# A two-stage image layer: offset matrices composed, k and v turned by VectorE, side work spread and a tile later, VectorE's large steps in halves

## The reference

```python
qkv  = conv1x1(layernorm(x), w_qkv)              # 3 x 128 channels
q, k, v = depthwise 3x3 filters of qkv           # w_dw, b_dw
for g in range(4):                               # groups of 32 channels
    y      = concat(conv3x3(q[:32], pconv_off_w[g]), q[32:])     # "pconv"
    off[g] = conv1x1(y, w_off[g], b_off[g])      # 9 taps x (dy, dx)
mask = sigmoid(conv1x1(pconv(q, pconv_mask_w), w_mask, b_mask))  # 9 taps
# per point, group and tap: k and v at (y + ky + dy, x + kx + dx), bilinear
# from 4 corners, times mask; then attention of q over the 9 taps, w_proj, + x
```

## Time and profile before

| | |
|---|---|
| time, median of 3 runs | 9839.31 us (9834.57 to 9847.19) |
| the profiled execution's own time | 9855.23 us |
| its span, first to last instruction | 9853.4 us |
| busy PE / DVE / ACT / POOL | 3062.5 / 5717.2 / 1524.3 / 4639.8 us |
| first stage (`first_layers` up to the last tile) | 0 to 7035 us |
| gathers issued (L512) | 4608, 4583.7 us busy |
| granted TensorE clock, mean | 0.637 of full speed |

### The profile page before, as it was taken

How to read it: one execution, slowest core, us unless ns; L and a number is a source line. 1 busy time by engine, 2 the same in 40 slices (tenths; PEclk the granted TensorE clock), 3 DMA queues, 4 the chain that set the end, 5 groups by cost and what they waited for, 6 DMA issues and landing times. The chain is left out here.

```text
span 9853.4 us, 106326 instructions
## 1 busy us (share of the span) xinstructions
PE 3062.5 (31%) x41476; PEld 2212.3 (22%) x41476; DVE 5717.2 (58%) x6511; ACT 1524.3 (15%) x3478; POOL 4639.8 (47%) x4747
## 2 busy tenths in 40 slices
PE   3102101021001001021001100111245476899997
PEld 2000000000001000010000000000224365788885
DVE  6486574765754456765754455544574465555554
ACT  1000000000000000000000000100122132444442
POOL 0776677665777557766777566765200000000000
PEclk7556555555555555555555555555577788999998
DMA  4433345332453224333453234332221532222224
GB/s 86 121 107 98 88 115 145 105 93 85 117 147 99 83 83 124 102 103 90 114 150 99 80 89 117 102 91 74 52 44 71 162 93 82 71 67 64 67 67 176
DMA packets 822918, 966.47 MB, mean 98 GB/s; under 512 B 283029, under 2 KB 643561, under 8 KB 817897
## 3 DMA queue, kind: packets, MB, share of 16 engines
q0 software_dynamic: 221184, 604.27, 20.7%
q1 hardware_dynamic: 573880, 321.25, 13.3%
q10 hardware_dynamic: 27440, 34.87, 1.0%
HBM read 797.64 MB, written 155.99 MB: 97 GB/s over the span
## 5 line engine op out<-in xcount | busy, mean ns | idle before, releaser
L512 POOL DMA_INDIRECT l_rec<-records,l_row x4608 | 4583.7, 995 | 2384.4 <-issue 1423.6
L673 PE MATMUL l_pso<-l_id,l_att_t 128*128 128x128 f32 x128 | 60.8, 475 | 4714.6 <-DVE l_att_t L1074 2549.4
L1056 DVE TENSOR_TENSOR l_rec<-l_rec,l_psv 128x4608 f32<-128x4608 f32 x128 | 634.0, 4953 | 1044.7 <-DMA l_rec<-records,l_row 892.4
L673 PEld LDWEIGHTS l_pso<-l_id,l_att_t 128*128 128x128 f32 x128 | 23.3, 182 | 4781.9 <-DVE l_att_t L1074 2585.9
L1074 DVE TENSOR_REDUCE l_att_t<-l_rec 128x128 f32<-128x4608 f32 x128 | 1004.2, 7845 | 4.4
L2329 DVE COPY l3p_mix<-l3p_ps 128x512 f32<-128x512 f32 x1024 | 659.8, 686 | 576.6 <-PE l3p_ps L2205 576.6
L2291 ACT ACTIVATE l3p_mix<-l3p_ps 128x512 f32<-128x512 f32 x1024 | 556.7, 596 | 663.9 <-PE l3p_ps L2205 663.9
L1057 DVE TENSOR_REDUCE l_psv<-l_rec 128x144 f32<-128x4608 f32 x128 | 635.0, 4961 | 4.4
L1072 DVE TENSOR_TENSOR l_rec<-l_rec,l_psv 128x4608 f32<-128x4608 f32 x128 | 634.0, 4953 | 6.0 <-issue 1.6
L2205 PE MATMUL l3p_ps<-l3p_psi,l3p_ms 32*128 32x128 f32 x16384 | 612.4, 283 | 21.2 <-DVE l3p_mix L2329 16.6
L2166 POOL COPY l3p_four<-l3p_fil 128x128 f32 (+1 forms) x64 | 18.7, 293 | 1198.9 <-PE l3p_psm L2258 1197.8
(11 more groups left out here) (358 smaller groups left out, 6120.4 us busy)
## 6 DMA issues: line engine op xcount, KB each, us to landing
l_rec<-records,l_row POOLq DMA_INDIRECT x4608
l2b_w<-l_w SPq DMA_DIRECT2D x32, 1024.0 KB, 10.9
records<-l_area SPq DMA_DIRECT2D x48, 512.0 KB
l_row<-meta SPq DMA_DIRECT2D x124, 154.0 KB
l_x_hat<-l3a_xout ACTq DMA_DIRECT2D x32, 512.0 KB, 4.4
l3p_xin<-l_x_hat SPq DMA_DIRECT2D x128, 128.0 KB, 3.1
l_y_raw<-l3p_yr SPq DMA_DIRECT2D x64, 256.0 KB, 3.0
l3p_yin<-l_y_raw SPq DMA_DIRECT2D x128, 128.0 KB, 2.9
```

The costliest lines, as they stand in the source:

```text
L512: pool.indirect_dma_start(out=rec[:, r, c % HT, :], out_offset=None, in_=records[b].rearrange("r c d -> r (c d)"), in_offset=bass.Indirect ...
L1056: step(dve.tensor_tensor(keys, keys, asked.broadcast_to([P, GROUPS, TAPS * CORNERS, HC]), ALU.mult))
```

## The change

- **Offset matrices.** The weights of the 3x3 convolution come in another layout (`wt_s`, `wt_m`), are multiplied once on TensorE by the 1x1 matrices (`effect`, `we_s`), and a job offc is now three matmuls with the composed matrix on the shifted q and one on q. off4 and offm are gone. offs is a transposing job in batch 0 too.
- **Blocks turned by VectorE.** k and v are no longer transposed by TensorE and copied by ScalarE; one VectorE transpose of 32 x 32 blocks each, over 128 x 4096 elements (`blocks_of`), writes `kv_t`. A partition then holds one x of 32 for a group of channels, and `keep` stores from 32 partitions (was 64) in a transfer, with pieces of the same 256 bytes.
- **At most two jobs a slot** in points (one slot, number 20, has three). PG is 46, LG 39.
- **A tile later.** ScalarE takes jobs two slots after TensorE; on TensorE the projection of tile t - 1 comes behind the value sum of tile t; ScalarE's `turned` is of t - 1 and its store of t - 2; VectorE adds t - 2 and waits for the transpose of t - 1 in its place; SP loads the residual a turn later. linear's own steps move by one or two slots.
- **Halves of 18.** Each large step of VectorE is two, over two groups of channels (18 of the 36 records). GpSimd waits for each half of the values by itself before it issues 18 gathers.

```diff
-        opening = [("qkv", (f, g), 5 + f) for f in range(3) for g in range(NG)]
...
-        beside = [("qkv", (f, g), 5 + (NG * f + g) // 6) for f in range(3) for g in range(NG)]
-        beside += [("qt", g, 18 + g // 3) for g in range(NG)]
-        beside += [("off4", g, 21 + g // 3) for g in range(NG)] + [("offm", g, 21 + (NG + g) // 3) for g in range(NG)]
-        beside += [("offc", g, 28 + g // 4) for g in range(NG)] + [("offs", g, 30 + g // 4) for g in range(NG)]
-        beside += sorted([("kt", g, 39 + g // 2) for g in range(NG)] + [("vt", g, 38 + g) for g in range(NG)], key=lambda j: j[2])
+        alone = [("qkv", (f, g), 5 + f) for f in range(3) for g in range(NG)]
+        alone += [("qt", g, 17) for g in range(NG)] + [("offc", g, 20) for g in range(NG)] + [("offs", g, 28) for g in range(NG)]
+        beside = [("qkv", (f, g), 5 + (NG * f + g) // 2) for f in range(3) for g in range(NG)]
+        beside += sorted([("qt", g, 17 + g // 2) for g in range(NG)] + [("offc", g, 20 + g) for g in range(NG)], key=lambda j: j[2])
+        beside += [("offs", g, 28 + g // 2) for g in range(NG)]
...
-                    y0 = 1 - dy + half
-                    dst = cells_of(b)[g, y0:y0 + H - 1:2, 1:1 + W, dy, :].rearrange("t x d -> x t d")
-                    src = kept[W * half:W * half + W, :, g, :, :].rearrange("p t a d -> p t (a d)")
+                    x0 = 1 + HC * half
+                    dst = cells_of(b)[g, 1 - dy:1 - dy + H, x0:x0 + HC, dy, :].rearrange("y x d -> x y d")
+                    src = kept[HC * g:HC * g + HC, half:NT * CORNERS:2, :, :].rearrange("p y a d -> p y (a d)")
...
-                if 2 <= t < TILES + 2:
-                    r = t - 2
+                if t >= 3:
+                    r = t - 3
...
             for b in range(BATCH):
                 with pool.Fori(max(1, b * NT // AHEAD), (b + 1) * NT // AHEAD) as i:
                     for s in range(AHEAD):
                         hold(pool, s_row[s], 16 * i + 16, s_gate[1])
-                        hold(pool, s_dve, AHEAD * STEPS * (i - 1) + summed(s + 2), s_gate[1])
-                        gather(b, s)
+                        for h in range(2):
+                            hold(pool, s_dve, AHEAD * STEPS * (i - 1) + summed(s + 2, h), s_gate[1])
+                            half(b, s, h)
...
                             for dy in range(3):
-                                last = pe.matmul(bank[0:m, :], wp_s[:, dy, o:o + m], pads[0][0:3 * HC, 8 * at + dy:8 * at + dy + 8, 0:W],
-                                                 start=dy == 0, stop=dy == 2)
...
+                                pe.matmul(o, we_s[:, dy, :], pads[0][0:3 * HC, 8 * at + dy:8 * at + dy + 8, 0:W], start=dy == 0, stop=False)
                             last = pe.matmul(o, wc_s[:, :], q_img[:, at * 512:at * 512 + 512], start=False, stop=True)
...
                 pe.wait_ge(s_dve, summed(t))
+                if t >= 1:
+                    project(t - 1)
                 pe.transpose(ps_a, att_t[t % 2][:, :], id_s[:, :]).then_inc(s_att, 1)
-                project(t)
...
-                        if own + int(b >= 1 and kind != "qkv") != slot or kind == "offs":
+                        if own + 2 * int(b >= 1) != slot or kind == "offs":
...
                 weigh(t)
+                if t >= 2:
+                    store(t - 2)
                 if t >= 1:
-                    store(t - 1)
-                turned(t)
+                    turned(t - 1)
...
+                def blocks_of(f):
+                    kept = kv_t if b else kv_t0
+                    dve.transpose(kept[:, :, f - 1, :], img[f].rearrange("p (j s) -> p j s", s=HC)).then_inc(a_blk, 1)
...
-                    for f, at in ((0, 10), (1, 18), (2, 37)):
+                    for f, slots in ((0, range(9, 17)), (1, range(18, 26)), (2, (30, 31, 32, 33, 39, 40, 41, 42))):
...
+                    if slot == 43 and b:
+                        dve.wait_ge(a_mst, b * 32 + 32)
+                        blocks_of(1)
+                    if slot == 44 and b:
+                        blocks_of(2)
...
             def add(t, step):
-                dve.wait_ge(s_proj, t + 1)
+                if t + 1 < TILES:
+                    dve.wait_ge(s_att, t + 2)
+                else:
+                    dve.wait_ge(s_proj, t + 1)
...
                 for h in range(2):
+                    keys = view[h][:, :, :, 0:HC]
+                    asked = ps_q[:, HG * HC * h:HG * HC * (h + 1)].rearrange("p (g o d) -> p g o d", o=1, d=HC)
                     dve.wait_ge(s_rec[2 * two + h], 16 * HT * (t // 2 + 1))
-                step(dve.tensor_tensor(keys, keys, asked.broadcast_to([P, GROUPS, TAPS * CORNERS, HC]), ALU.mult))
+                    step(dve.tensor_tensor(keys, keys, asked.broadcast_to([P, HG, TAPS * CORNERS, HC]), ALU.mult))
...
-                if t >= 1:
-                    add(t - 1, step)
+                if t >= 2:
+                    add(t - 2, step)
...
+                for h in range(2):
+                    values = view[h][:, :, :, HC:2 * HC]
+                    part = ps_w[:, HT * CORNERS * h:HT * CORNERS * (h + 1)].rearrange("p (g m) -> p g m", g=HG)
+                    step(dve.tensor_tensor(values, values, part.unsqueeze(3).broadcast_to([P, HG, TAPS * CORNERS, HC]), ALU.mult))
+                    dve.tensor_reduce(att_t[two][:, HG * HC * h:HG * HC * (h + 1)].rearrange("p (g d) -> p g d", g=HG),
+                                      values.rearrange("p g m d -> p g d m"), AX, ALU.add).then_inc(s_dve, 1)
```

More of the change, by code:

```diff
@@ L334, in taken, with after @@
             return sum(1 for j in jobs[:n] if j[0] != "offs")
-        def after(jobs, kind):
-            return max(n for n, j in enumerate(jobs) if j[0] == kind) + 1
+        def after(jobs, kind, at=NG - 1):
+            return [j[0:2] for j in jobs].index((kind, at)) + 1
         lj = [("x", g, 3 + g // 3) for g in range(NG)] + [("k", g, 10 + g // 4) for g in range(NG)]
@@ L571, in points @@
                             for t in range(4):
                                 i = 4 * at + t
-                                last = pe.transpose(bank[:, t * P:t * P + P], src[:, i * P:i * P + P], id_s[:, :])
-                        if kind in ("off4", "offm"):
+                                last = pe.transpose(bank[:, t * P:t * P + P], q_img[:, i * P:i * P + P], id_s[:, :])
+                        if kind == "offc":
                             if at == 0:
                                 pe.wait_ge(a_shift, b * 48 + 64)
-                            m, o = (P, 0) if kind == "off4" else (HC, P)
+                                pe.wait_ge(a_eff, 1)
+                            o = bank[0:OFFS, :]
@@ L578, in points @@
                             for dy in range(3):
-                                last = pe.matmul(bank[0:m, :], wp_s[:, dy, o:o + m], pads[0][0:3 * HC, 8 * at + dy:8 * at + dy + 8, 0:W],
-                                                 start=dy == 0, stop=dy == 2)
-                        if kind == "offc":
-                            pe.wait_ge(a_act, done_act + taken(pj, after(pj, "offm")))
-                            o = bank[0:OFFS, :]
-                            pe.matmul(o, wa_s[:, :], conv4[:, at * 512:at * 512 + 512], start=True, stop=False)
+                                pe.matmul(o, we_s[:, dy, :], pads[0][0:3 * HC, 8 * at + dy:8 * at + dy + 8, 0:W], start=dy == 0, stop=False)
@@ L585, in points @@
                             last = pe.matmul(o, wc_s[:, :], q_img[:, at * 512:at * 512 + 512], start=False, stop=True)
-                        if kind == "offs" and b:
-                            pe.wait_ge(a_act, done_act + taken(pj, pj.index(("offc", at, 28 + at // 4)) + 1))
+                        if kind == "offs":
+                            pe.wait_ge(a_act, done_act + taken(pj, after(pj, "offc", at)))
                             for t in range(4):
@@ L590, in points @@
                                 last = pe.transpose(bank[:, t * P:t * P + OFFS], conv4[0:OFFS, i * P:i * P + P], id_s[0:OFFS, 0:OFFS])
-                        if kind == "offs" and not b:
-                            pe.wait_ge(a_act, done_act + taken(pj, after(pj, "offm")))
-                            for t in range(4):
-                                i = 4 * at + t
-                                o = bank[:, t * P:t * P + OFFS]
-                                pe.matmul(o, conv4[:, i * P:i * P + P], wa_s[:, :], start=True, stop=False)
-                                last = pe.matmul(o, q_img[:, i * P:i * P + P], wc_s[:, :], start=False, stop=True)
                         last.then_inc(a_job, 1)
@@ L743, in linear @@
                     for n, (kind, g, own) in enumerate(lj):
-                        if own + 1 != slot:
+                        if own + 2 != slot:
                             continue
```

236 lines of the change are left out of this document (120 added, 116 removed).

## The result

The changed kernel takes 9594.93 us in the median of 4 runs (9577.43 to 9633.59), the kernel before 9841.13 (9834.57 to 9847.19) beside it: ratio 0.9755, 95% interval 0.9725 to 0.9786. It is faster, by 2.45%. Forecast were 9490 us and a gain of 353; the medians give 246. The profiled execution took 9595.74 us with a span of 9593.5, so 260 us of span went, against 353 forecast.

What follows compares the result with a forecast made beforehand. GpSimd's gathers bound the first stage, with waits on VectorE from TensorE's per-instruction pace. Terms of -300, -110, +10, +70, +2 and -25 sum to -353, giving 9502 profiled and 9490 us as median; 8 in 10: 9220 to 9700.

Steps and rivals of the forecast that it cites:

- What bounds the kernel: First stage: GpSimd's gathers set a floor of 45.0 us a tile, 5760 us; TensorE's slow jobs hold VectorE up.
- Composed matrices and turned blocks, two a slot: Points batches: less TensorE work per tile cuts GpSimd's waits from 359.6 to 60 us, -300, bounds -150 and -360.
- Halves: Linear batches: GpSimd's next gather released 6.4 us earlier at each of 18 waits, 115 us, booked as -110.
- Everything a tile later in linear: Linear batches: better order but the same TensorE work, so given nothing; bounds 0 and -280.
- Four more steps a tile: VectorE's split steps cost 0 to 0.8 us a tile, partly hidden by idle time: +10, up to +97.
- What the faster VectorE uncovers: Gathers stopped beside VectorE's side steps and block transposes, in three batches: +70, bounds 0 and +107.
- rival C: GpSimd's gathers take 1.40 us instead of 1.25 when issued without pauses: +113, 9950 us; chance 0.06.
- Block transposes: Two a batch on VectorE, about 4.4 us each, up to 7.85; without a lock +55 instead of +70.
- Start: Before the first gather: two transposes, 8.8 us instead of 6.9, +2, up to +9; stores at worst +25.
- End: After the last gather: the last tile needs some 25 us instead of 65; -25, bounds 0 and -40.
- A: TensorE's pace came from ping-pong with ScalarE, so all 744.8 us of waits go: 9150 us; chance 0.15.
- B: TensorE stays the bound in points and linear batches; waits move to VectorE's `add`: -123, 9715 us; chance 0.23.

Runs made afterwards that it cites:

- six_a_slot_b: Changed kernel with the qkv jobs six a slot again, where the kernel before took 9845.58 us: 9606.72 us, ratio 0.9755.
- whole_steps_b: Changed kernel with VectorE's four large steps a tile whole again, where the kernel before took 9837.7 us: 9593.91 us, ratio 0.9745.
- six_a_slot: Changed kernel with the qkv jobs six a slot again, where the kernel before took 8867.17 us: 8867.81 us, ratio 1.0000.
- tiles_alone: Changed kernel with other batches' side work moved behind the tiles, gathering batch 0's records only, where the kernel before took 8867.17 us: 10022.92 us.
- after_again: The changed kernel, unchanged, run once more where the kernel before took 9845.0 us: 9625.38 us, ratio 0.9764.
- before_again: The kernel before, unchanged, run once more for its trace where the kernel before took 9845.0 us: 9842.85 us, ratio 1.0001.
- tiles_alone_b: Changed kernel with other batches' side work moved behind the tiles, gathering batch 0's records only, where the kernel before took 9837.7 us: 10677.24 us.

## Why the prediction was right in direction and 105 us off

The time fell into the likeliest case's range (9350 to 9620), in part by luck: the waits in the points fell by 60 us more than forecast, those in the linear batches by the size forecast but not for the reason given, and the gathers cost three times their term (238 against 80). On a chip B no run of a variant gained anything. By its own steps:

- **What bounds the kernel: half right.** TensorE's slow jobs under gathers do hold VectorE up on chips A. But the floor of 45.0 us a tile, 5760 us in all, was read from the median gather, and on a chip A it is not reachable: with everything else taken away the gathers need 6421. Before stood 330 us above that (6751.1), after stands 94 above it (6515.2). Even 6421 is no hard floor: pauses earn pace back, so waits and pace can't simply be added to it.
- **Composed matrices and turned blocks, two a slot: -300.** The points' waits went from 359.6 us to nothing, the end of the bounds (-360). The offc tiles, feared for 45 to 67 us of jobs, wait nowhere. Undoing the two jobs a slot for qkv brings no wait back (six_a_slot_b), so the cause is the smaller work, the tile of slack, the spreading of the other jobs, or several of these; the two runs that were to tell the first two apart met the other kind of chip.
- **Halves: -110, measured 0.** This is the term that failed. The linear waits did fall by 385.2 - 270.9 = 114.3, the size forecast, but they stand at 270.2 with whole steps too (whole_steps_b), so it wasn't the halves. And a shorter wait would not have shortened the stage by its length: on a chip A pauses of 24 us are paid back to nine tenths (671 of 747 us). I had priced the earlier release at its full length, and not asked what a pause gives.
- **Everything a tile later in linear: 0.** By elimination the 114 us belong here or to the work taken away; no run shows which.
- **Four more steps a tile: +10.** With whole steps the time is the same, within some 20 us, and the run takes away gain and cost together. The instructions themselves cost what was bounded: two half steps take 5.10 us for 4.95 (L1068, L1056) and 8.00 for 7.85 (L1089, L1074), 0.15 us each, some 0.6 a tile. VectorE's idle time, with 1525.7 us of waits for the gathers' data, can cover that.
- **What the faster VectorE uncovers: +70, measured +238** (183.8 busy, 53.8 gaps). The term was for stops by VectorE's steps with two SBUF operands. Those exist: L1016, the L1007 of before, has a gather of 4.60 us beside it. On chips B the longer gathers of six_a_slot add only about 50 us over tiles_alone. The rest is the pace, which rival C had (0.15 us on each of up to 4608 gathers) and which I gave 0.06. C's sum failed because it let every gather pay: with the remaining 270.9 us of pauses to its credit the excess ended at 225 + 238 = 463, below the 578 at which C decides. The earlier trace rows had both paces. The stretch at 0.94, from 4734 us, came behind waits of 31.1 and 44.2 us that end at 4407 and 4631 in the trace of before: I took it as evidence against C, and it fits the credit.
- **Block transposes: sized right, and not a stop.** 4.43 us each. Beside one, from 1243.14 to 1247.59 us in six_a_slot, the gathers keep to 0.95, as beside its five others:

```profile
1244.18 0.95 POOL L521 DMA_INDIRECT l_rec<-records,l_row  x1 [0.30 <-issue]
1245.43 0.95 POOL L521 DMA_INDIRECT l_rec<-records,l_row  x1 [0.30 <-issue]
```

and beside L1016 (from 3504.10 to 3508.51 us) in the profile after one doesn't:

```profile
3504.73 4.60 POOL L521 DMA_INDIRECT l_rec<-records,l_row  x1 [0.30 <-issue]
```

By the rule of the Trainium skill (SBUF — State Buffer, section "SBUF: two separate sides") only a step with two SBUF inputs, and that against a GpSimd instruction that reads SBUF, or one in a two-port mode, takes the shared ports. The trace agrees for the transpose and for L1016; on two-port modes it has nothing. All longer gathers on a chip B together are 48.7 us, so the +55 that the rule gave was nearer than +70, and still high; the rule says nothing of the pace.

- **Start: +2, measured -9.5** (217.3 to 207.8). The sixteen stores of the records from 32 partitions are issued in 41.4 us where the earlier trace rows has 50.0, and in 41 to 43 in every other run of the new form; I had bounded this change of shape at nothing or worse, and it was a gain. The order of the cells in DRAM changed too, so the number of partitions alone isn't shown to be the cause.

```profile
160.48 41.41 SPq L426 DMA_DIRECT2D records<-l_rec  x16
```

- **End: -25, not settled.** From the last gather's start to the end of the last value step there were 65.7 us, and the profile after has 36.7, which is -29. But after_again has 82.8 and six_a_slot_b 80.2, more than before (65.2 in before_again), while whole_steps_b has 34.7. In after_again VectorE still has steps of linear (L1022 to L1024, up to 6753 us) ahead of the last two tiles when the last gather starts at 6733.7. The bounds 0 and -40 were too narrow. To the end of the span it is 2885.0 us before and 2870.5 after, which is less than the same stretch varies between runs.

Why 474 us of waits less were worth 236, the traces let one estimate. Let every gather at 1.25 us take 0.143 us (1.394 less 1.251) out of a store, let GpSimd's waits and stops of over 2 us fill it, and let a gather be slow when it is empty. If the store holds at most 22 us, a value fitted to the trace of before, this gives 222 us of lost pace there, where the distance from first to last gather holds 220 beyond 1.251 us a gather and these waits and stops; in the profile after it gives 442 where there are 450. Without a limit it gives 30 and 377. So waits like the 42 to 54 us of before are paid back only in part, and those were worth taking away. No run varied the length of a pause to test this.

Together: -473.9 + 183.8 + 53.8 = -236 on the gathers, -9.5 at the start, -14.5 behind the last gather's start, -260.

Of the rivals, A (all waits go) is wrong on a chip A, where 270.9 us stay. B (the waits only move) saw the place rightly, but for the wrong batches: VectorE now stops in the addition, where L1049 waits for the transpose (by the code; the profile names no record for it), 516 us in all.

```profile
L1049 DVE TENSOR_TENSOR l_done<-l_pso,l_res 128x128 f32<-128x128 f32 x128 | 37.3, 291 | 518.8 <-remote 515.9
```

All of it stands in the three windows of the linear batches (170.6, 173.6 and 171.7 us), whose 271 us of GpSimd's waits lie there too. In the points L1049 waits 0.6 us in all, so the offc tiles that B feared hold up nothing. D (no change) is wrong.

What is not settled is the condition itself. On chips A, while gathers run, GpSimd averages 1.39 us a gather where it doesn't pause, and TensorE takes 4.9 us or more for a job that takes 0.86 us on chips B; the stages behind it take about the same on both (2841 to 2906 us from the last gather in the kernels with their side work in place). The gathers' data land as soon on both (the last packet 2.36 to 2.43 us after the issue, tile by tile in the median, in tiles_alone and tiles_alone_b from the third tile on), and the instruction queue moves the same 324 packets, so neither later landings nor more fetches are seen. No experiment was made on it, and the cause stays open.

## What to carry to other kernels

Before a wait is priced at its length, look at what the engine does right behind it: where its instructions run faster after a pause than in unbroken work (1.25 against 1.40 us here), the wait is in part credit, and only an experiment that adds pauses to a bare loop tells how much. Take the floor of a stage from a run of that loop with all else removed, not from the median instruction. And a tuning won on one chip may be worth nothing on the next: 2.45% here, while four variants of the changed kernel made no difference on the other kind of chip (ratios 0.9990 to 1.0009).

## What the runs showed of the hardware that was not expected

- The same kernel takes 9838 to 9846 us on some chips and 8867 to 8871 on others. Of the 771 us between the profiled spans of six_a_slot and six_a_slot_b, one program, 709 lie between the first and the last indirect gather.
- GpSimd's gathers of 128 records: 1.251 us from start to start on one kind of chip, 1.394 on the other once about five tiles (180 gathers) have been issued, with 746.7 us of pauses costing 75 us.
- A transpose by blocks of 128 x 4096 float32 takes 4.43 us on VectorE and leaves the gathers beside it at 0.95 us (six_a_slot), where L1016, with two SBUF operands and 4.41 us, holds one for 4.60.
- Sixteen stores of 512 KB with the same pieces of 256 bytes are issued in 41.4 us from 32 partitions and in 50.0 from 64, with another order of cells in DRAM.
